# A feed-forward stage interleaved with the attention of the next two batches, in bursts

## What is computed

```python
def cond(x, mask, Wq, Wk, Wv, b):                 # x [8, 256, 512]
    Q, K, V = (einsum('oc,bct->bto', W, x) split into 16 heads of 16 for W in (Wq, Wk, Wv))
    att = einsum('bhqd,bhkd->bhqk', Q, K) / 4 + b[0]
    att = softmax(att * m + (1 - m) * -1e30)       # m: mask of the keys
    return einsum('bhqk,bhkd->bhqd', att, V) as [8, 256, 512]
def ffn(y, ...):                                   # y as 2048 rows of 512
    Wg, Wu, Wd = dequant(4-bit codes, one scale for 32)   # 512 x 4096, 512 x 4096, 4096 x 512
    gate, up = y @ Wg.T, y @ Wu.T
    g = 0.5 * gate * (1 + tanh(0.7978845608 * (gate + 0.044715 * gate ** 3)))
    return (g * up) @ Wd.T
out = x + ffn(cond(x, mask, Wq, Wk, Wv, b), ...)
```

## Time and profile before

| | |
|---|---|
| median of 3 runs | 1612.29 us (1604.95 to 1619.18) |
| the profiled execution | 1610.11 us, its span 1608.3 us |
| PE, DVE, ACT, POOL busy | 94%, 43%, 33%, 17% of the span |
| attention | to about 603 us |
| FFN | from there to the end |
| mean granted clock of PE | 0.937 of 2.4 GHz |

### The profile page before, as it was taken

One profiled execution on the slowest core, in us unless ns is written; L12 is line 12 of the kernel. 1 busy time (PEld: TensorE's weight loads), 2 busy tenths in 40 slices (PEclk: granted clock), 3 DMA queues, 4 the chain that ended last, 5 costly groups with the idle time before them and its releaser, 6 DMA issues.

```text
span 1608.3 us, 19482 instructions
## 1 busy us (share of the span) xinstructions
PE 1510.4 (94%) x7376; PEld 597.7 (37%) x7376; DVE 695.6 (43%) x1113; ACT 534.6 (33%) x701; POOL 270.4 (17%) x146
## 2 busy tenths in 40 slices
PE   3989889898989889999999999999999999999999
PEld 1222222222322224444444444444444444444444
DVE  5858676776777562323323233323233232122122
ACT  1447464564656463222222222222222222111111
POOL 2012112121211212122112212211221221000000
PEclk7779896897898899999999999999999999999999
DMA  5112221212221103001001000100100010000000
GB/s 165 44 51 59 65 63 43 61 44 57 67 69 42 51 21 124 20 20 40 20 20 33 26 20 20 39 20 20 36 23 20 20 39 1 0 26 26 0 26 26
DMA packets 32662, 63.04 MB, mean 39 GB/s; under 512 B 5584, under 2 KB 14928, under 8 KB 32480
## 3 DMA queue, kind: packets, MB, share of 16 engines
q1 hardware_dynamic: 29760, 59.42, 12.5%
q10 hardware_dynamic: 2848, 2.90, 0.5%
HBM read 49.43 MB, written 12.61 MB: 39 GB/s over the span
## 4 chain that ended last, share of the span: by engine, by line
PE 82%; DMA 6%; DVE 5%; SPq 3%; ACT 2%; issue 1%; ACTq 1%; POOL 1%; POOLq 0%; DVEq 0%
PE psum L828 14%; PE psum L830 14%; PE psum L829 14%; PE psum L769 7%; PE psum L899 7%; PE psum L901 7%; PE psum L900 7%; PE psum L798 6%; DMA wide<-seed_rows 4%; DVE maxima L638 3%; PE psum L784 3%; PE psum L756 2%; PE psum L805 1%; PE psum L746 1%; DMA wide<-max_lo 1%
## 5 line engine op out<-in xcount | busy, mean ns | idle before, releaser
L638 DVE TENSOR_REDUCE maxima<-psum 128x1 f32<-128x512 f32 x512 | 332.3, 685 | 161.9 <-PE psum L769 158.3
L703 DVE SCALAR_TENSOR_TENSOR small<-psum,small 128x512 f32<-128x512 f32 x128 | 88.5, 691 | 592.6 <-issue 306.6
L544 ACT ACTIVATE big<-psum 128x1024 f32<-128x1024 f32 x256 | 253.4, 1024 | 214.8 <-PE psum L784 198.2
L769 PE MATMUL psum<-wide 51*128 51x512 f16 x512 | 211.3, 447 | 68.3 <-DMA wide<-seed_rows 51.1
L580 ACT ACTIVATE small<-psum 128x512 f32<-128x512 f32 x128 | 76.4, 597 | 421.1 <-PE psum L830 421.1
L334 POOL TENSOR_TENSOR dq_w<-dq_code,dq_scales 128x1536 f32<-128x1536 f16 x32 | 109.8, 3433 | 541.8 <-DVE dq_code L371 541.8
L590 ACT CAST in_hi<-small 128x512 f16<-128x512 f32 x128 | 79.1, 618 | 361.8 <-DVE small L703 361.8
L828 PE MATMUL psum<-y_hi,wide 128*128 x512 | 194.1, 379 | 2.6 <-POOL wide L346 2.6
L828 PE MATMUL psum<-y_hi,w_even_hi 128*128 (+1 forms) x512 | 194.2, 379 | 1.2 <-POOL w_even_lo L346 1.2
L829 PE MATMUL psum<-y_lo,w_even_hi 128*128 (+1 forms) x512 | 194.0, 379 | 0.0
L830 PE MATMUL psum<-y_hi,w_even_lo 128*128 (+1 forms) x512 | 194.0, 379 | 0.0
(11 more groups left out here) (83 smaller groups left out, 1366.2 us busy)
## 6 DMA issues: line engine op xcount, KB each, us to landing
dq_packed<-packed SPq DMA_DIRECT2D x32, 384.0 KB
dq_scales<-scales SPq DMA_DIRECT2D x32, 384.0 KB
wide<-qk_parts SPq DMA_DIRECT2D x64, 128.0 KB
qk_parts<-wide SPq DMA_DIRECT2D x60, 128.0 KB
small<-x SPq DMA_DIRECT2D x8, 512.0 KB, 4.1
wide<-qk_parts SPq DMA_DIRECT2D x64, 64.0 KB
big<-x SPq DMA_DIRECT2D x4, 1024.0 KB, 9.5
out<-big SPq DMA_DIRECT2D x16, 256.0 KB, 2.1
```

The costliest lines, as they stand in the source:

```text
L544: nc.scalar.activation(p_exp[:, k, :, i], p_score[:, 2 * i:2 * i + 2, :], ACT.Exp, scale=SCORE_SCALE).then_inc(exp_done, 1)
L638: nc.vector.reduce_max(maxima[:, g % 2, n:n + 1], p_max[:, n % 2, :], AX.X).then_inc(max_red, 1)
L769: nc.tensor.matmul(p_max[:, n % 2, :], q_stack[rows, side, s, t * P:(t + 1) * P], k_stack[rows, side, s, :], start=True, stop=True).then_i ...
```

## The change

The FFN no longer waits for all of attention. Its order is turned round: four chunks of 512 rows (two batches each), and in each all 32 units. `schedule()` is one list that all engines follow. Batches 0 and 1 run alone by `PLAN`. From the `YN` of batch 2's first quad on, which completes the rows of chunk 0, the FFN steps of chunk c are dealt out between the attention steps of the next two batches; chunk 3 runs alone. An FFN step (`G0` to `U3`, `D`) is three matmuls. `SHARED_PLAN` has eight `|` marks a quad; at each one an equal share of the chunk's 384 steps is placed, six steps or 18 matmuls (five at first in chunk 0, which has 368). What stands between two marks is a burst: one score step, two max tiles, and one or two other steps.

What goes with it:
- Down projections are gathered: after unit 4m+4 the four row blocks of units 4m to 4m+3 are multiplied one after the other, 48 matmuls (steps `D`), and each is added into `acc`, which now holds one chunk; it is loaded and stored once a chunk, the first load near the start of the kernel.
- Weights: chunk 0 decodes units 2 to 31 while it uses them, two units ahead, and writes each to DRAM; chunks 1 to 3 read them back (0.79 MB a unit, three units ahead) into a ring of 8. Packed codes and scales have two buffers; decode steps 1 to 3 reuse the code buffers.
- PSUM: scores have one pair of banks instead of two; gate and up have one bank each until unit 96, and the down projections use the same two banks in turn until then.
- Two max tiles are reduced by one DVE instruction over 1024 columns, and the two tiles come from different halves of the rows.
- Gelu becomes Square on ACT, a product on DVE (`cubic`), Tanh on ACT, a second product on DVE, and the product with up; the low part of the result moves to GpSimd (`inter_low`).
- All loops of the FFN are written out.

```diff
-GROUPS = 4
-UNITS = F // P // GROUPS
+UNITS = F // P
+GROUP = 4
 CHUNKS = B * C // 512
+STEPS = CHUNKS * UNITS
+RING = 2 * GROUP
+IN_RING = GROUP + 1
+AHEAD_UNITS = 2
+LAST_CHUNK = (CHUNKS - 1) * UNITS
+LAST_SHARED = LAST_CHUNK // GROUP - 1
+SOLO = 2
+GELU_A = 0.044715
+GELU_B = 0.7978845608028654
 WORDS = 2 * P + 2 * P + 256
...
+        def gate_bank(u):
+            return psum[:, 0 if u > LAST_CHUNK and u % 2 else 2, :]
+        def up_bank(u):
+            return psum[:, 1 if u > LAST_CHUNK and u % 2 else 3, :]
+        def out_bank(j, r):
+            return psum[:, 2 + r % 2 if j < LAST_SHARED else 4 + r, :]
...
+        SHARED_PLAN = (
+            "S00 m m A2 V1a | S01 m m A3 V1b | V1h AO S10 m m | MT Y S11 m m | MH XH ML YN S20 A0 m m | "
+            "MV S21 m m Q0a | S30 A1 m m Q0b | Q0h S31 Q0l m m |",
+            "X S00 m m A2 K0a | S01 m m A3 K0b | K0h AO S10 K0l m m | MT Y S11 m m | MH ML YN S20 A0 m m | "
+            "MV S21 m m Q1a | S30 A1 m m Q1b | Q1h S31 Q1l m m |",
+            "S00 m m A2 K1a | S01 m m A3 K1b | K1h AO S10 F0 K1l m m | MT Y S11 m m | MH ML YN S20 A0 m m | "
+            "MV S21 m m V0a | S30 A1 m m | S31 m m |",
+            "S00 m m A2 V0b | V0h S01 m m A3 | AO S10 m m | MT Y S11 m m | MH ML YN S20 A0 m m | MV S21 m m | "
+            "G1 S30 A1 m m | S31 m m |",
+        )
...
+        def schedule():
+            steps = list(attention())
+            ready = [n + 1 for n, (b, g, step, _) in enumerate(steps) if step == "YN" and g == 0 and b >= 2 and b % 2 == 0]
+            for b, g, step, arg in steps[:ready[0]]:
+                yield "attention", b, g, step, arg
+            for c in range(CHUNKS):
+                rest = list(ffn(c))
+                span = steps[ready[c]:ready[c + 1]] if c < CHUNKS - 1 else []
+                left = sum(step == "|" for _, _, step, _ in span)
+                for b, g, step, arg in span:
+                    yield "attention", b, g, step, arg
+                    if step == "|":
+                        count = len(rest) // left
+                        left -= 1
+                        for u, name, part in rest[:count]:
+                            yield "ffn", u, None, name, part
+                        rest = rest[count:]
+                for u, name, part in rest:
+                    yield "ffn", u, None, name, part
...
+            load_rows(sp, 0)
+            for kind, b, g, step, arg in schedule():
+                if kind == "ffn":
+                    u, c = b, b // UNITS
+                    if step == "G0" and u < STEPS:
+                        if u + AHEAD_UNITS + 1 < UNITS:
+                            load_unit(sp, u + AHEAD_UNITS + 1)
+                        if UNITS <= u + AHEAD_UNITS + 1 < STEPS:
+                            reload_unit(sp, u + AHEAD_UNITS + 1)
...
+            def inter_low(u):
+                wait_apart(pool, pool_spare, in_hi_s, u + 1)
+                nc.gpsimd.tensor_tensor(in_lo[:, u % IN_RING, :], inter[:, :], in_hi[:, u % IN_RING, :],
+                                        ALU.subtract).then_inc(in_lo_s, 1)
+            for kind, b, g, step, arg in schedule():
+                if kind == "ffn":
+                    u = b
+                    if step == "G1" and u:
+                        inter_low(u - 1)
+                    elif step == "G3" and SOLO <= u + AHEAD_UNITS - 1 < UNITS:
+                        weight_lo(pool, u + AHEAD_UNITS - 1)
+                    elif step == "U2" and u + AHEAD_UNITS < UNITS:
+                        weight_f(pool, u + AHEAD_UNITS)
...
+            def square(u):
+                act.wait_ge(gate_mm, u + 1)
+                wait_from(act, inter_s, u - 1)
+                nc.scalar.activation(gelu[:, u % 2, :], gate_bank(u), ACT.Square,
+                                     scale=GELU_A ** 0.5 / (Y_SCALE * W_SCALE)).then_inc(square_s, 1)
+            def tanh(u):
+                act.wait_ge(cubic_s, u + 1)
+                nc.scalar.activation(gelu[:, u % 2, :], gelu[:, u % 2, :], ACT.Tanh,
+                                     scale=GELU_B / (Y_SCALE * W_SCALE)).then_inc(tanh_s, 1)
...
+            def inter_high(u):
+                act.wait_ge(inter_s, u + 1)
+                if u >= IN_RING:
+                    act.wait_ge(sum_mm, 4 * ((u - IN_RING) // GROUP + 1))
+                nc.scalar.copy(in_hi[:, u % IN_RING, :], inter[:, :]).then_inc(in_hi_s, 1)
...
+                        weight_hi(act, u + AHEAD_UNITS - 1)
+                    elif step == "G3":
+                        square(u)
+                    elif step == "U1":
+                        tanh(u)
...
+            def reduce_pair(b, g, n):
+                q = 4 * b + g
+                if n == 0:
+                    wait_from(dve, max_t, q - 1)
+                dve.wait_ge(max_mm, 16 * q + n + 2)
+                nc.vector.reduce_max(maxima[:, g % 2, n // 2:n // 2 + 9:8], p_max, AX.X).then_inc(max_red, 2)
...
+            def cubic(u):
+                dve.wait_ge(square_s, u + 1)
+                nc.vector.scalar_tensor_tensor(out=gelu[:, u % 2, :], in0=gelu[:, u % 2, :], scalar=1.0,
+                                               in1=gate_bank(u), op0=ALU.add, op1=ALU.mult).then_inc(cubic_s, 1)
+            def gelu_part(u):
+                dve.wait_ge(tanh_s, u + 1)
+                nc.vector.scalar_tensor_tensor(out=gelu[:, u % 2, :], in0=gelu[:, u % 2, :], scalar=1.0,
+                                               in1=gate_bank(u), op0=ALU.add, op1=ALU.mult).then_inc(gelu_s, 1)
+            def inter_part(u):
+                dve.wait_ge(gelu_s, u + 1)
+                dve.wait_ge(up_mm, u + 1)
+                wait_from(dve, in_lo_s, u)
+                nc.vector.scalar_tensor_tensor(out=inter[:, :], in0=up_bank(u),
+                                               scalar=0.5 * I_SCALE / (Y_SCALE * W_SCALE) ** 2,
+                                               in1=gelu[:, u % 2, :], op0=ALU.mult, op1=ALU.mult).then_inc(inter_s, 1)
+            def add_rows(j, r):
+                dve.wait_ge(sum_mm, 4 * j + r + 1)
+                if j % (UNITS // GROUP) == 0:
+                    dve.wait_ge(acc_in, 16 * (j // (UNITS // GROUP)) + 16)
+                else:
+                    dve.wait_ge(acc_add, 4 * (j - 1) + r + 1)
+                nc.vector.scalar_tensor_tensor(out=acc[:, r, :], in0=out_bank(j, r), scalar=1.0 / (I_SCALE * W_SCALE),
...
+            for kind, b, g, step, arg in schedule():
+                if kind == "ffn":
+                    u, n = b, b + AHEAD_UNITS
+                    if step == "G1" and n < UNITS:
+                        decode(dve, n, 0)
+                    elif step == "G2" and n < UNITS:
+                        decode(dve, n, 1)
+                    elif step == "G3" and n < UNITS:
+                        decode(dve, n, 2)
+                    elif step == "U0":
+                        cubic(u)
+                    elif step == "U1" and n < UNITS:
+                        decode(dve, n, 3)
+                    elif step == "U2":
+                        gelu_part(u)
+                    elif step == "U3":
+                        inter_part(u)
+                    elif step == "D" and arg[2] == GROUP - 1:
+                        add_rows(arg[0], arg[1])
...
+                if b_now < SOLO or n % 2 == 0:
+                    wait_from(pe, max_red, 16 * (4 * b + g) + n - (1 if b_now < SOLO else 0))
+                e, i, t = n % 2, n // 8, n // 2 % 4
...
+                wait_from(pe, exp_done, n - 1 if b < SOLO else n)
+                bank = 2 * i if b < SOLO else 0
...
+            def wait_bank(u, used, freed):
+                if u > LAST_CHUNK:
+                    wait_from(pe, freed, u - 1)
+                elif u > GROUP and u % GROUP == 1:
+                    pe.wait_ge(acc_add, 4 * (u // GROUP - 1) + used + 3)
                 else:
...
+            def down(j, r, i):
+                u = GROUP * j + i
+                if i == 0:
+                    if r == 0:
+                        pe.wait_ge(in_lo_s, GROUP * j + GROUP)
+                    if j > LAST_SHARED:
+                        pe.wait_ge(acc_add, 4 * (j - 1) + r + 1)
+                    elif j < LAST_SHARED:
+                        if r < 2:
+                            pe.wait_ge((gelu_s, inter_s)[r], GROUP * j + GROUP + 1)
+                        else:
+                            pe.wait_ge(acc_add, 4 * j + r - 1)
+                slot = u % RING - u % 2
+                w_hi, w_lo = (w_ring[:, slot:slot + 2, p, u % 2, 4 * P:4 * P + 256] for p in range(2))
+                dst, rows, s = out_bank(j, r), slice(r * P, (r + 1) * P), u % IN_RING
+                nc.tensor.matmul(dst, in_hi[:, s, rows], w_hi, start=(i == 0), stop=False)
+                nc.tensor.matmul(dst, in_hi[:, s, rows], w_lo, start=False, stop=False)
+                last = nc.tensor.matmul(dst, in_lo[:, s, rows], w_hi, start=False, stop=(i == GROUP - 1))
+                if i == GROUP - 1:
```

(51 more changed lines are left out.)

505 lines of the change are left out of this document (235 added, 270 removed).

## The result

The changed kernel takes 1676.22 us (1670.75 to 1677.24), the one before 1614.82 us on the same chip: a ratio of 1.038, 95% interval 1.033 to 1.044. It is slower, by about 61 us, and lies above the predicted range. Its profiled execution has a span of 1669.0 us.

A forecast was written before the change was run, and what follows sets the result against it. PE was taken as the bound: FFN matmuls at their floor, only attention's 600 us could shrink. The sum 215 + 992 + 245 + 27 + 68 + 12 + 7 = 1566 us of span was scaled to 1570 us, range 1528 to 1645.

The forecast's parts named there:

- step 3: Attention still to do once the FFN starts: 23.5 quads at 10.9 us, after corrections 245 us.
- step 5: Decoding in chunk 0: GpSimd waits out DVE's decode steps, not the reverse; 9.5 us a quad, 68 us in all.
- Start: Everything before the first FFN matmul: 215 us, with 4 for the accumulator load and 2 for the burst's rest.
- FFN matmuls: All 4608 matmuls of the FFN, already at their floor: 992 us.
- The prediction's own sign: Chunks 1 and 2 over 370 us each would mean the gelu chain or attention bursts are mis-sized, not the decode.
- The gelu chain: One gate bank up to unit 96, free only after the second gelu product: 27 us over chunks 1 and 2.
- Fills and the y split: Waits for stack fills, 5 us over five batches, and for y splits before chunks' first gates, 7: 12 us.
- The end: Last low part before the last down projections, and the time after the last matmul's start: 7 us.
- B: Rival for chunk 0: DVE decode steps and GpSimd work each wait for the other; 1592 to 1634 us, chance 0.3.
- A: Rival for chunk 0: DVE and GpSimd hardly hinder each other, 31 us instead of 68; 1533 us, chance 0.2.
- C: Rival: Tanh and Exp reload the table, 95 to 140 us more; 1665 to 1710 us, chance 0.08 with D.
- D: Rival: each burst waits 0.5 us for an exp or transpose, 94 us; 1665 us, chance 0.08 with C.

The follow-up runs named there:

- one input: Changed kernel with DVE's four decode steps from unit 2 on replaced by equally long row maxima over one SBUF input; 1605.99 us, 0.994 of the kernel before.
- spread, YN earlier: Changed kernel with decoding of units 2 to 31 spread over the FFN steps and MH ML YN one burst earlier; 1569.91 us, 0.974 of the kernel before.

## Why the prediction was wrong

Its own sum was 1566 us of span; 1669 was measured. Three errors of like size make the miss: the attention work (step 3), the conflict and the clock in chunk 0 (step 5), and a wait that the sum doesn't have. By these figures, taking away any one of them leaves the kernel slower than before. By its steps:

1. **Start.** 209.2 instead of 215: the price put on the accumulator load wasn't there (-6), nor the rest of the burst.
2. **FFN matmuls.** Right: 18 of them with the switch take 4.0 us at full clock, as counted.
3. **Attention.** Mis-sized by 36 us (281 instead of 245). Without its waits chunk 1 takes 346.8 us, PE's busy time there; less 384 x 0.646 = 248 us for the FFN that is 12.3 us a quad, not 10.9. The prediction's own sign for this (chunks over 370 us) is what chunk 1 shows. An A step costs 1.0 us, not 0.5: the row read for it, `x8` and 1.07 us long, is one step of eight matmuls (1024 of L798 over 32 quads of four steps), and I took it for two. A V piece costs less, 0.68 instead of 1.28: the row read for it lies in a stretch with a granted clock of 0.50. By chunks: 99 in chunk 1, 83 in chunk 2 by the same subtraction, and taken as 99 for chunk 0, which has the same steps.
4. **The gelu chain** in chunks 1 and 2. Right in place and size: 22 us, 27 predicted, and 16 of its 21 pauses are at the gate of unit 4m+3, the one that needs unit 4m+2's release.
5. **Chunk 0.** The step that failed. It let the port conflict act in one direction only, GpSimd waiting for DVE, because no row showed the other. The runs show both. Waits on gelu alone are 66.4 us. Another 37 is what PE's busy time of 373.2 us has beyond 238 of FFN and 99 of attention; I put it down to matmuls at the lower clock: 113 FFN matmuls that start over 0.3 us after the one before, with no wait between, account for 23 of it (1 us in chunk 1, where the distance is 0.215), and the rest is inferred. That is 103 in all against the 68 (+35). The clock was put down at nothing, "since PE no longer pauses for long"; with 35 pauses of 2.7 us in the mean and up to 5.5 (94 us) the granted clock was 0.90. The kernels with less waiting in chunk 0 have 0.95 (one input, 46 us), 0.98 (spread, YN earlier, 44 us) and 0.99 (no decoding, 26 us).
6. **Fills and the y split.** Small, as said: 3.1 us of fills in chunk 0, and with the splits 7.3, 5 us under the sum.
7. **The end.** Right within 1 us.

**Missed altogether** was the wait of A0 for YN: 23.6, 12.0 and 10.4 us in the three chunks, 46 in all. It needed no unknown price. The plan has YN ahead of A0 in one burst, and DVE's order puts YN behind two gelu products; I costed DVE's delay only for the gate bank and never asked who waits for YN. -6 + 36 - 5 + 35 + 46 - 5 + 1 = 102 of the 103 us. That this closes is no proof of the parts: the 36 and the 37 in step 5 are remainders after the waits were taken off.

**The rivals.** B, both ways, is what happened: it forecast 417 to 460 us for chunk 0 and decode steps of over 1 us, and the steps take 1.3 to 1.6 us; chunk 0 is longer still (467), with 23.6 us of the missed wait in it. B's time, 1592 to 1634, is missed too, by 42 us, since it shares the sum's other terms. It was given 0.3 and should have had more. The Trainium skill (SBUF — State Buffer, SBUF: two separate sides) spoke for it: where a DVE operation with two SBUF inputs or in a two-port mode meets a GpSimd operation, the one that starts first holds the shared port to its end. The trace agrees both ways (steps that wait 2.2 us for a low part; an in_lo that waits 0.45 for a step). Row maxima over one input, for which the page names no such lock, run in 946 and 551 ns beside a running GpSimd. A is excluded by the steps' durations, C by the single table load in the groups (tanh and exp do share a set here), D by PE's waits: none on an exp in the chunks.

The claim that DVE "would fit" rested on busy shares. In chunk 0 DVE is busy 345 of 467 us, still not the bound: what counts is where its instructions stand.

## What to carry to other kernels

When one engine's queue serves two interleaved pipelines, write down for each instruction that frees a buffer what stands ahead of it there, and its worst duration; do so for every bank, not only for the largest. Before decoding on DVE and GpSimd is put under a latency-bound chain, assume that either can hold the other for most of an instruction, and place them apart. When several such delays share a stretch, the first one removed may gain nothing; try the edits together before one of them is dropped.
